# Feed-forward, second sweep: product and largest negative in one VectorE instruction; largest positive from the largest gate, found in the first sweep

## The reference, cut to what matters

```python
x    = act_qdq(x)
up   = act_qdq(x @ lpbq_dequant(w_up).T)
gate = act_qdq(x @ lpbq_dequant(w_gate).T)
sig  = fixed_qdq_u16(jax.nn.sigmoid(gate))     # multiples of 1/65536
gate = act_qdq(gate * sig)                     # needs max |gate * sig|
o    = act_qdq(gate * up)                      # needs max |gate * up|
return o @ lpbq_dequant(w_down).T
```

## Time and profile before

| What | us |
|---|---|
| Median of three runs (2003.05 to 2006.66) | 2003.8 |
| The profiled execution's own time | 2003.72 |
| Its span, first to last instruction | 2001.6 |
| First sweep (about) | 1435 to 1562 |
| Second sweep (about) | 1563 to 1729 |
| Third sweep (about) | 1731 to 1859 |

### The profile page before, as it was taken

One profiled execution on the slowest core, in us unless ns is written; L12 is line 12 of the kernel. 1 busy time (PEld: TensorE's weight loads), 2 busy tenths in 40 slices (PEclk: granted clock), 3 DMA queues, 4 the chain that ended last, 5 costly groups with the idle time before them and its releaser, 6 DMA issues. The chain is left out here.

```text
span 2001.6 us, 70719 instructions
## 1 busy us (share of the span) xinstructions
PE 1860.6 (93%) x28023; PEld 1309.7 (65%) x28023; DVE 1582.8 (79%) x2870; ACT 1197.2 (60%) x2015; POOL 418.0 (21%) x516
## 2 busy tenths in 40 slices
PE   6999999999999968999999999999699988899798
PEld 4667666677666656888888888887344333344687
DVE  6777777777777765888888888887465799988897
ACT  4455444445444425777777777776355666688465
POOL 1112212211111121323232323232000222100121
PEclk9999999999999979999999999999699999899899
DMA  4111111111111011212121212120288788599574
GB/s 142 41 35 35 45 40 34 40 45 34 40 40 40 24 53 51 60 48 58 47 58 47 58 47 59 46 60 5 74 268 274 274 313 313 193 404 384 190 270 148
DMA packets 169444, 221.90 MB, mean 111 GB/s; under 512 B 80691, under 2 KB 142390, under 8 KB 169270
## 3 DMA queue, kind: packets, MB, share of 16 engines
q1 hardware_dynamic: 169270, 219.22, 33.0%
HBM read 116.40 MB, written 94.37 MB: 105 GB/s over the span
## 5 line engine op out<-in xcount | busy, mean ns | idle before, releaser
L1535 PE MATMUL ff_twin<-ff_xq,w_uh 128*128 (+1 forms) x1152 | 347.7, 384 | 38.4 <-DVE ff_top L1904 24.0
L1535 PEld LDWEIGHTS ff_twin<-ff_xq,w_uh 128*128 128x128 f16 x1152 | 111.1, 99 | 187.9 <-issue 43.9
L1535 PE MATMUL ff_twin<-ff_xq,w_ul 128*128 (+1 forms) x576 | 220.5, 383 | 0.0
L721 DVE TENSOR_TENSOR x<-rec_x,rec_until 128x512 f32<-128x512 f32 x256 | 159.0, 683 | 50.8 <-PE rec_x L401 50.8
L573 ACT ACTIVATE x<-rec_e,rec_hidden 128x512 f32<-128x512 f32 x256 | 158.0, 687 | 55.7 <-PE rec_e L418 55.7
L307 POOL TENSOR_TENSOR rec_o<-rec_tmp 128x512 f32<-128x512 f32 x32 | 68.2, 2131 | 561.9 <-DVE rec_tmp L771 561.9
L1266 DVE TENSOR_REDUCE mneg<-att_s 128x4 f32<-128x512 f32 x256 | 158.8, 682 | 26.8 <-PE att_s L1037 26.8
L541 ACT ACTIVATE rec_v<-rec_f 128x256 f32<-128x256 f32 x64 | 24.5, 383 | 213.7 <-DVE rec_z L730 213.7
L1183 ACT ACTIVATE att_e<-att_s 128x512 f32<-128x512 f32 x256 | 132.2, 612 | 21.3 <-PE att_s L1070 21.3
L748 DVE TENSOR_TENSOR rec_tmp<-rec_x,x 128x512 f32<-128x512 f32 x128 | 79.7, 683 | 82.4 <-POOL rec_o L309 70.0
L430 PE MATMUL rec_x<-x 32*32 32x64 f32 x8192 | 139.1, 218 | 4.2 <-issue 3.9
(11 more groups left out here) (245 smaller groups left out, 4436.1 us busy)
## 6 DMA issues: line engine op xcount, KB each, us to landing
raw_scratch<-ff_out SPq DMA_DIRECT2D x32, 768.0 KB, 3.5
ff_in<-raw_scratch SPq DMA_DIRECT2D x32, 768.0 KB, 5.9
gate_scratch<-ff_out SPq DMA_DIRECT2D x28, 768.0 KB, 3.5
ff_in<-gate_scratch SPq DMA_DIRECT2D x28, 768.0 KB, 9.1
product_scratch<-ff_out SPq DMA_DIRECT2D x28, 768.0 KB, 8.7
ff_out<-product_scratch SPq DMA_DIRECT2D x28, 768.0 KB, 5.9
turned_scratch<-rec_xT SPq DMA_DIRECT2D x32, 256.0 KB, 2.9
att_x<-in_x SPq DMA_DIRECT2D x32, 256.0 KB, 2.8
```

Source lines behind the costliest of these rows:

```text
L721: V.tensor_tensor(mt[:, b].rearrange("p (a j m) n -> p j a m n", a=KC, m=2)[:, j], X[j].rearrange("p (a m n) -> p a m n", a=KC, m=2), unti ...
L1535: m = T.matmul(bank_.rearrange("p (b n) -> p b n", b=BT), weights(wp, kc, a, c), tile[:, xp, :, kc], start=(i == 0), stop=(i == len(terms) ...
```

## The change

- VectorE's second sweep has one instruction per half, `opposite`: it writes minus the product and gives, per partition, the largest of these values and 0. That is the largest magnitude among the negative products. `product` and `largest` stay for the third sweep, with the sign put back through the factor K_2.
- The largest positive product: x times sigmoid(x) grows with x for x above 0, so it comes from the largest gate. `highest_signed`, a new VectorE maximum of each half in the first sweep, finds it; six values per partition are then rounded, put through the sigmoid on ScalarE, made whole on GpSimd and multiplied on VectorE.
- `integers` for tiles 2 to 15 moves from VectorE to GpSimd.
- The last tile's two `highest_signed` run after `scale_of(1, 1)`, at the start of the second sweep; the sigmoid of tiles with u = 1 waits for them.
- The sigmoid no longer waits for `largest` (`maxed`).
- VectorE's order in `sweep2` becomes: highest 0, opposite 0, highest 1, highest 2, opposite 1.
- SyncE's order becomes: refill half 1, store half 0, refill half 0 of the next tile, store half 1.
- The second sweep's loops on VectorE and SyncE are written out tile by tile.

```diff
+                def integers(n, s):                      # now on GpSimd
+                    pool.wait_ge(q1["low"], n - 1)
+                    G.tensor_scalar(xi[:, s], t["x2"][...], one(R_X), 1.0, ALU.mult, ALU.mult).then_inc(q1["whole"], 1)
+                for n in range(2, NT):
+                    integers(n, n % 2)
...
+                def highest_signed(n, u, s):
+                    V.tensor_reduce(signed[:, s * HC:(s + 1) * HC, bass.ds(n, 1)].rearrange("p c a -> p (c a)"),
+                                    ob[:, u, s].rearrange("p (c n) -> p c n", c=HC), AX.X,
+                                    ALU.max).then_inc(q1["peaks"], 1)
...
-                    act.wait_ge(q["maxed"], 2 * m + s + 1)
+                    if u == 1:
+                        act.wait_ge(q1["peaks"], 4 + NG)
...
+                act.wait_ge(q1["peak"], 3)
+                A.activation(crest_s[:], crest_i[:], ACT.Sigmoid, scale=one(S_G)).then_inc(q["sourced"], 1)
...
+                pool.wait_ge(q["sourced"], 2 * NT + 1)
+                G.tensor_scalar(crest_u[:], crest_s[:], I_MULT, 0.0, ALU.mult, ALU.add).then_inc(q1["row"], 1)
...
+                def opposite(m, u, s):
+                    dve.wait_ge(q["fixed"], 2 + 2 * m + s + 1)
+                    V.tensor_tensor_reduce(ob[:, u, s], whole[:, u, s], fixed_u[:, s], -1.0, 0.0, ALU.mult, ALU.max,
+                                           topg[:, 2 * m + s:2 * m + s + 1]).then_inc(q["prod"], 1)
...
                 def sweep2(m, u, n):
-                    for s in range(2):
-                        product(m, u, s, fixed_u)
-                        highest(m + 1, n, s)
-                    largest(m, m, u, 0)
+                    highest(m + 1, n, 0)
+                    opposite(m, u, 0)
+                    highest(m + 1, n, 1)
                     highest(m + 1, n, 2)
-                    largest(m, m, u, 1)
+                    opposite(m, u, 1)
...
-                        refill(2 * j + u, 2 * j + u + 3)
-                        for s in range(2):
-                            store(g_d, 2 * j + u, 2 * j + u + 2, u, s)
+                    refill(m, (m + 3) % NT, 1)
+                    store(g_d, m, m + 2, u, 0)
+                    refill(m + 1, (m + 4) % NT, 0)
+                    store(g_d, m, m + 2, u, 1)
```

More of the change, by code:

```diff
@@ L1594, in _ @@
                         sp.wait_ge(raw_out[u][s], 16 * (1 + NT // 2))
-                with sp.Fori(0, NT // 2 - 2) as j:
-                    for u in range(2):
-                        refill(2 * j + u, 2 * j + u + 3)
-                        for s in range(2):
-                            store(g_d, 2 * j + u, 2 * j + u + 2, u, s)
[L1600 to L1604, removed]
+                refill(0, 3, 0)
+                for m in range(NT - 2):
+                    u = m % 2
+                    refill(m, (m + 3) % NT, 1)
+                    store(g_d, m, m + 2, u, 0)
+                    refill(m + 1, (m + 4) % NT, 0)
+                    store(g_d, m, m + 2, u, 1)
+                refill(NT - 2, 1, 1)
                 for s in range(2):
@@ L1842, in share, with over_partitions @@
                     G.tensor_scalar(fixed_u[:, s], ob[:, u, s], I_MULT, 0.0, ALU.mult, ALU.add).then_inc(q["fixed"], 1)
-                with pool.Fori(0, NT // 2) as j:
+                def over_partitions(k):
+                    pool.wait_ge(q["part"], k)
+                    nc.gpsimd.partition_all_reduce(topa[:, 0:1], top1[:, 0:1], P, RMAX).then_inc(q["all"], 1)
+                with pool.Fori(0, NT // 2 - 1) as j:
                     for u in range(2):
@@ L1847, in _ @@
                             share(2 * j + u, u, s)
[L1848 to L1852, removed]
+                for s in range(2):
+                    share(NT - 2, 0, s)
+                for s in range(2):
+                    share(NT - 1, 1, s)
+                pool.wait_ge(q["sourced"], 2 * NT + 1)
+                pool.sem_inc(q["seen"], 1)
+                G.tensor_scalar(crest_u[:], crest_s[:], I_MULT, 0.0, ALU.mult, ALU.add).then_inc(q1["row"], 1)
+                for k in (2, 3, 4):
+                    over_partitions(k)
                 def power(p, u):
@@ L1960, in _, with product @@
                     highest(0, 2, k)
-                def product(m, u, s, other):
-                    dve.wait_ge(q["fixed"], 2 + 2 * m + s + 1)
-                    dve.wait_ge(q["maxed"], 2 * m + s + 1)
-                    V.tensor_tensor(ob[:, u, s], whole[:, u, s], other[:, s], ALU.mult).then_inc(q["prod"], 1)
+                for s in range(2):
+                    highest_signed(NT - 1, 1, s)
+                dve.wait_ge(q1["peaks"], 4 + NG)
+                v.did(V.tensor_reduce(crest[:], signed[:], AX.X, ALU.max))
+                v.wait()
+                v.did(V.tensor_tensor(crest_i[:], crest[:], cf[:, FC:2 * FC], ALU.mult))
+                v.wait()
+                dve.sem_inc(q1["peak"], 1)
+                def opposite(m, u, s):
+                    dve.wait_ge(q["fixed"], 2 + 2 * m + s + 1)
+                    V.tensor_tensor_reduce(ob[:, u, s], whole[:, u, s], fixed_u[:, s], -1.0, 0.0, ALU.mult, ALU.max,
+                                           topg[:, 2 * m + s:2 * m + s + 1]).then_inc(q["prod"], 1)
+                def product(m, u, s):
+                    dve.wait_ge(q["fixed"], 2 + 2 * m + s + 1)
+                    dve.wait_ge(q["maxed"], 2 * (m - NT) + s + 1)
+                    V.tensor_tensor(ob[:, u, s], whole[:, u, s], fixed_i[:, s], ALU.mult).then_inc(q["prod"], 1)
                 def largest(m, k, u, s):
@@ L1972, in sweep2 @@
                 def sweep2(m, u, n):
-                    for s in range(2):
-                        product(m, u, s, fixed_u)
-                        highest(m + 1, n, s)
-                    largest(m, m, u, 0)
+                    highest(m + 1, n, 0)
+                    opposite(m, u, 0)
+                    highest(m + 1, n, 1)
                     highest(m + 1, n, 2)
-                    largest(m, m, u, 1)
+                    opposite(m, u, 1)
                 def sweep2_last(m, u):
                     for s in range(2):
-                        product(m, u, s, fixed_u)
+                        opposite(m, u, s)
+                    dve.wait_ge(q1["row"], 3)
+                    v.did(V.tensor_tensor(topg[:, NG:NG + FC], crest_i[:], crest_u[:], ALU.mult))
                     scale_of(0, 2)
-                    for s in range(2):
-                        largest(m, m, u, s)
                 def sweep3(m, k, u, stores):
@@ L1990, in sweep3 @@
                         dve.wait_ge(stored[u][s], 16 * (stores + 1))
-                        product(m, u, s, fixed_i)
+                        product(m, u, s)
                     for s in range(2):
                         largest(m, k, u, s)
[L1995 to L1998, removed]
+                for m in range(NT - 1):
                     sweep2(m, m % 2, (m + 3) % NT)
```

44 lines of the change are left out of this document (27 added, 17 removed).

## The result

| | before | after |
|---|---|---|
| median of the runs | 2003.42 us (2001.91 to 2006.66) | 1986.64 us (1984.06 to 1989.56) |
| ratio, 95% interval | | 0.9928 [0.9911, 0.9946] |
| profiled execution, its span | 2003.72, 2001.6 | 1984.42, 1982.7 |
| first rounding of the raw gate to first rounding of up (the second sweep) | 164.8 | 149.6 |
| one gate tile, third to sixteenth | 10.005 | 8.97 |

The kernel is 0.7% faster: 16.8 us by the medians, 19.3 between the two profiled executions, where 31 were forecast. Of the 19.3, 15.2 lie in the second sweep, 2.7 before it and 1.1 behind it (the rest is outside the span).

What follows compares the result with a forecast made beforehand. VectorE was taken to bound only the second sweep, TensorE the first and third. Start and tiles -31.1, step to the third sweep +0.3 and -0.2, sum -31.0 on 2003.72 us: forecast 1973, range 1969 to 1988.

Steps and rivals of the forecast that it cites:

- The fused instruction: Second sweep, VectorE: product with maximum takes 1.82 us a half, replacing 1.67 + 1.66; VectorE then 7.03 a tile.
- Rival C: Second sweep: fused instruction at half rate with read-out, 3.45 us a half; +6, 2010 us; chance 0.05 slower, 0.03 unchanged.
- Rival D: First sweep becomes VectorE's: unoverlapped semaphore waits bring its list to 8.13 us a tile; +5, 1978 us; chance 0.06.
- The start: Start of second sweep: third gate tile begins at 1583.0 instead of 1585.48, 2.5 us earlier.
- The step to the third sweep: Second to third sweep: GpSimd's gap before its maximum stays; +0.3 for the crest work, -0.2 for ScalarE's earlier level.
- the loop: Second sweep, single buffer per half: rounding 1.97 plus landing 5.9 gives 7.87 us; tile taken at 7.8, saving 28.7.
- Rival B: Second sweep: refills land in 6.4 to 7.3 us, tile 8.4 to 9.3; 8 to 20 back, 1981 to 1993; chance 0.17.

Runs made afterwards that it cites:

- x8_small_stores: Changed kernel with only the first third of each product stored in the second sweep, the third sweep loading the raw gate instead; 1971.85 us, single execution.
- x2: Changed kernel with each half's refill split into three 256 KB transfers, each issued once its third is rounded; 1972.76 us, ratio 0.9851 to the kernel before.
- x3: Changed kernel with refills from the third tile on sent elsewhere in SBUF and ScalarE not waiting for them; 1966.31 us, single execution.
- x5: Changed kernel with each refill in two transfers, 256 KB after the first third's rounding and 512 KB after the last; 1971.33 us, ratio 0.9861 to the kernel before.
- x6: Changed kernel with refills issued from ScalarE's own DMA queue, SyncE keeping only the stores; 1991.77 us, ratio 0.9954 to the kernel before.
- x9: The changed kernel with refills in two pieces, repeated on another chip with more rounds; 1971.21 us, ratio 0.9847 to the kernel before.
- x7: Kernel before with only SyncE's new order in the second sweep; 2005.45 us, ratio 1.002 to the kernel before.
- x1: The changed kernel run again, unaltered, beside the kernel before; 1988.53 us, ratio 0.9919.
- x11: Changed kernel with two-piece refills, plus the last tile's two shares and the crest's moved from GpSimd to VectorE; 1959.1 us, ratio 0.9802 to the kernel before.

## Why the prediction was right and wrong

**Held.** The fused instruction costs what the plain product did. In the second sweep of the kernel after:

```profile
1693.62 1.76 DVE L2003 CUSTOM_DVE_ANT_0 ff_out<-ff_whole,s_other 128x1536 f32<-128x1536 int16 x1 [0.84 <-POOL s_other L1856]
1695.31 0.08 DVE L2003 DVE_READ_ACCUMULATOR2_ANT ff_topg<- 128x1 f32 x1
1695.31 2.35 DVE L1926 TENSOR_REDUCE ff_top<-ff_twin 128x2 f32<-128x1024 f32 x2
```

1.76 us against 1.74 in the earlier trace rows, and the next one starts 1.69 behind its start (1.82 forecast): the read-out exists, 0.08 us, and lies wholly beside its neighbours. Rival C is out. The rule behind it, half throughput for two sources in SBUF that aren't bfloat16 (the Trainium skill, "Vector Engine (DVE) Microarchitecture Reference", "Points that are easy to get wrong"), is stated for one layout of instructions. This instruction, CUSTOM_DVE_ANT_0 in the trace, has two sources of 16-bit integers in SBUF and doesn't show it; whether it has that layout no run says.

Rival D is out too. VectorE in the first sweep, the rows that answer to the earlier trace rows:

```profile
1446.46 1.75 DVE L1939 TENSOR_REDUCE ff_top<-ff_out 128x1536 f32 x1 [0.43 <-ACT ff_out L1673]
1448.13 0.68 DVE L1921 TENSOR_TENSOR s_low<-s_whole,s_high 128x1024 f16<-128x1024 int16 x1
1448.73 1.75 DVE L1932 TENSOR_REDUCE ff_signed<-ff_out 128x1536 f32 x1
1450.40 1.75 DVE L1939 TENSOR_REDUCE ff_top<-ff_out 128x1536 f32 x1
1452.06 1.75 DVE L1932 TENSOR_REDUCE ff_signed<-ff_out 128x1536 f32 x1
1454.23 1.75 DVE L1939 TENSOR_REDUCE ff_top<-ff_out 128x1536 f32 x1 [0.43 <-ACT ff_out L1673]
```

One tile later is 7.77 us later, with 0.43 us to spare in it (0.46 forecast). GpSimd's integers took 1.12 us, 1.0 estimated. The start: the third gate tile comes 16.6 us after the first rounding, 18.7 before; 16.2 was forecast. The step to the third sweep went as said (16.4 us from the last gate tile to the first rounding of up, 16.0 before); GpSimd, in rows that answer to the earlier trace rows:

```profile
1706.16 0.21 POOL L1872 TENSOR_SCALAR ff_crest_other<-ff_crest_sig 128x6 uint16<-128x6 f32 x1
1712.29 0.38 POOL L1860 PARTITION_ALL_REDUCE ff_topa<-ff_top  x1 [5.92 <-issue]
```

**Failed.** The step was: "A landing of 5.9 gives a loop of 7.87, a shorter one less", and with it "I take a tile at 7.8 us: TensorE's 7.77, with the loop just under it". The form of the loop was right and the landing in it was wrong: 6.8 (7.4 in the second run). ScalarE waited 1.9 us a tile for the raw gate where under 0.5 was forecast, and TensorE was busy 93% of the stretch where over 97% was. Even by its own figures the loop wasn't under the bound: 1.97 + 5.9 = 7.87 is 0.1 over TensorE's 7.77. ScalarE's timeline, the third gate tile and the last:

```profile
1580.69 1.95 ACT L1694 ACTIVATE ff_whole<-ff_in,ff_coef 128x512 int16<-128x512 f32 x3 [2.63 <-DMA ff_in<-raw_scratch]
...
1697.29 1.95 ACT L1694 ACTIVATE ff_whole<-ff_in,ff_coef 128x512 int16<-128x512 f32 x3 [0.18 <-DMA ff_in<-raw_scratch]
```

(1697.29 - 1580.69) / 13 = 8.97 us, 1.17 over 7.8; 13 x 1.17 = 15.2 us, which is nearly all of the 15.8 by which the sweep missed 133.8. The 5.9 was read in a kernel with 2 x (5.9 + 3.4) / 10.05 = 1.85 transfers in flight on average (3.4 is the landing of its stores, 1600 to 1690 us). I moved it unchanged into one that issues them faster, where 2 x (6.8 + 7.9) / 8.97 = 3.3 are in flight. These averages contain the landings themselves, so they describe the crowding and don't prove a cause. Read apart from them, in the stretch from 1590 to 1670 us: when a store was issued, 1.0 other transfers had not landed in the kernel before and 3.0 in the kernel after; for a refill it was 1.5 and 2.0. The experiment is x8_small_stores: with 2 x 5.5 + 2 x 4.1 / 3 (counted by bytes) in 7.82 us, 1.8 in flight, the landing is 5.5.

The kernel before did have a row at the rate that was aimed at. Its third sweep moves four transfers of the same size in each 7.77 us, and there (1770 to 1830 us) they land in 9.0 and 9.2 us:

```profile
product_scratch<-ff_out SPq DMA_DIRECT2D x15, 768.0 KB, 9.0
ff_in<-gate_scratch SPq DMA_DIRECT2D x15, 768.0 KB, 9.2
```

That sweep loads into two sets of buffers, so a long landing costs it nothing, and 9.2 is no forecast for the second sweep; but it says that landings over 7.3 were to be had at this rate. I used that sweep to say that the transfers keep up, and took 7.3 as the longest landing read.

**My argument against the rival** was that refills and stores are spread 2 to 3 us apart. SyncE's queue after, the rows that answer to the earlier trace rows:

```profile
1641.73 0.33 SPq L1563 DMA_DIRECT2D ff_in<-raw_scratch  x1
1642.16 0.37 SPq L1571 DMA_DIRECT2D gate_scratch<-ff_out  x1
1645.62 0.33 SPq L1563 DMA_DIRECT2D ff_in<-raw_scratch  x1
1646.87 0.34 SPq L1571 DMA_DIRECT2D gate_scratch<-ff_out  x1
1650.53 0.33 SPq L1563 DMA_DIRECT2D ff_in<-raw_scratch  x1
```

A store follows its refill by 0.4 to 1.3 us. The forecast's own times already had one such pair, the refill of half 0 at 9.7 and the store of half 1 at 10.3 or later; I compared the refill only with the store ahead of it. That a late refill, by making ScalarE late, pushes the two still closer is argued, not shown. Rival B is what happened: its 8.4 to 9.3 a tile and 1981 to 1993 us hold the first run (8.97, 1984.42), and its second run's tile (9.42) lies just over it. Its condition holds in part: the DMA share rose to 0.98, but TensorE wasn't full, and the rate, 354 GB/s, was under the 405 to 409 of x2 and x3. I gave it 0.17. The median, 1986.64, lies in the range of 1969 to 1988 only because that range reached into B: the time is covered, the mechanism of the forecast isn't. A loop 0.1 us over the bound at the one landing read in the steady stretch, and anywhere from 6.0 to 9.3 by the bounds given (4.0 and 7.3), was no more than an even bet.

**Shown and open.** Shown: the loop sets the sweep (x2, x3, x5), a limit of the transfers near 350 GB/s doesn't (405 to 409 GB/s with the same bytes), one queue for both kinds doesn't (x6), and the landing depends on the stores beside it (x8). With the loop under 7.77 us the sweep takes 134.3 to 135.0 us (x5, x8, x9), where the forecast had 133.8: everything else in the sum stood. Open: why the landing is 6.8 in one execution and 7.4 in the next; why the DMA share reads 0.98 at 354 GB/s and 1.03 at 409, that is, what the transfer engines spend their packets' time on when they move less; and why the landing fell to 6.4 in two pieces.

## What to carry to other kernels

A landing read in a trace belongs to the rate of that trace. When a change speeds a stage up and a single buffer is refilled behind its consumer, add the consumer's time to a landing read at the new rate, not at the old; another stage of the same kernel may have one (here the third sweep, 9.2 us, where the second then showed 6.8 to 7.4). If the sum isn't clearly under the bound, refill in pieces, which brought 15.8 us here (1972.76 against 1988.53 on one chip). Such moves are worth what the bound of the stage lets through: SyncE's new order cost 3.5 us without the fused instruction (1.0005 to 1.0036 of the time before), and with it the trace shows 4 us saved at the start of the sweep. Before trusting a difference of a few us between two kernels, look at the clock that their runs were granted.

## What the runs showed of the hardware

- A product with its maximum in one VectorE instruction cost 1.76 us for 128x1536 from two 16-bit tensors in SBUF, the plain product 1.74; reading the maximum out took 0.08 us and no time of its own.
- Of VectorE's product and GpSimd's share, when they overlap, the one that starts second gets longer: the product 1.74 to 2.21 us behind a share (x7), the share 1.47 to 2.43 behind a product. With refills aside, where VectorE was busy 80.00 of 80 us, the fused one took 2.12 us in the mean of the sweep and up to 2.99.
- A refill of 768 KB landed in 5.5 us with 1.8 transfers in flight (x8, by bytes), in 5.9 with 1.85 (before), in 6.9 with 3.0 (x6, from ScalarE's queue), in 6.8 with 3.3 (after) and in 7.4 with 3.5 (x1). The number in flight is worked out from the landings and the period.
- GpSimd's 6 to 7 us ahead of a maximum over partitions (5.92 after, 7.22 in x11) count from the end of its last ordinary instruction, whether or not the input is ready: 34 us behind that end, the maximum followed its input by 0.2 us. So they can be laid beside other work by ending that list sooner.
- Over 46 runs of the kernel before, 1993 to 2007 us long, a mean granted clock lower by 0.01 went with 11 us more.
